# Early periods written out per engine, two small moves at the end of even periods, and small loads issued by ScalarE

## The chip, the cores and the metric

The kernel runs on one core of a Trainium2 chip. The metric is the device time of one launch in microseconds (us). Engines are named as in the profile: PE is TensorE, ACT ScalarE, DVE VectorE, POOL GpSimd; SP only issues DMAs.

## What is computed

One decoder block over 16 sequences of 128 tokens with 128 features, in float32:

```
x = LN(x + mixer(x))        # projection to 3x128, causal convolution of 3 taps on each channel,
                            # k*v, causal convolution of 4 taps, q*(..), projection to 128
x = LN(x + xattn(x, ctx))   # self attention (16 heads of 64), LN, cross attention to ctx, LN,
                            # feed forward 128-512-128 with GELU, LN
x = LN(x + ffn(x))          # 16 experts for tokens 0 to 15, one shared network for the rest
```

Both attentions mask keys by one padding mask.

## The kernel before, in words

All work sits in two blocks of hand-written instruction lists, one list per engine; engines meet only through semaphores, and an engine runs its list strictly in order. `mixer_and_attentions` (L263) holds the mixer and both attentions, `feed_forward` (L1057) the rest. A matmul that must be exact runs as three (`mm_split`, L71) over a high and a low part, so each operand is first split: ACT writes the high part, DVE the low part by a subtraction.

The first block is a loop over **periods** `p`, the same loop in all four engines, from `FIRST = -9` to 32. Period p works on attention item p (self attention of sequence p, and from 16 on cross attention of sequence p-16): values `v_half(p)`, four `unit`s (two head pairs of queries or keys each, for two sequences at once, needed by items two periods ahead), `transposes(p-1)` of the probabilities, `out_proj(p-2)`, `scores(p+1)`, `p_v(p-1)`. ACT does `exps`, `q_out`, `v_out`, `ot_out`; DVE `maxima` (with the mask), `reciprocals`, `k_out`, `pt_out`, `residual`, `xT_low`; POOL `normalise`, `affine` and the powers that make inverse deviations.

The mixer works on pairs m = 0 to 7 of sequences and is spread over the same periods, by leads that `pair_of(p, lead)` (L341) turns into a pair:

```
PROJECT, CONVOLVE, OUTPUT, TRANSPOSE = 8, 6, 5, 4
```

So pair m is projected at p = 2m-8 and 2m-7 (`projection`, 9 matmuls for each of 3 parts, evicted by `projected` into `C`), convolved at p = 2m-6 (POOL `keys_values` the period before, DVE `inner_convolution` L841, POOL `gate` L996), sent through the output matmul at 2m-5 (`mixer_output`, DVE `mixer_residual` and `mixer_statistics`, POOL `mixer_deviation`, DVE `mixer_shift`), and normalised and transposed at 2m-4 (ACT `mixer_normal` L655, PE `x1_transposes` L543, ACT `x1_high`, DVE `x1_low` L883). `x1T` is what the units read. Pair 0 reaches its transposes at p = -4; the units begin at p = -2 and `scores(0)` (L455) stands at the end of p = -1. The weights of self attention are split at p = -5, -4 and -3, and the mask is cast on DVE at p = -2 (L928).

In an even period with a pair to convolve (p = 0, 2, 4, 6, 8 of the periods from 0 on) `inner_convolution` stands on DVE right after `normalise(p-3)` and ahead of the reciprocals and copies of the period, and `gate` on POOL ahead of the four `normalise(p, g)`. `mixer_residuals` (L1018) stands at the end of an odd period's list on POOL.

All loads but the mask's are issued by SP, in the order of L370 to L396.

## Time and profile before

| | |
|---|---|
| median of 3 runs | 538.31 us (537.59 to 538.4) |
| the profiled execution's own time | 538.34 us |
| its span, first to last instruction | 536.6 us |
| mean granted PE clock | 0.951 |
| scores(0) starts | 49.27 us |
| first exponential on ACT | 51.67 us |

The profiled execution lies 0.03 us from the median, and 1.74 us of its time are outside the span. Times of rows count from the span's start. "[0.43 <-DVE at_k L758]" behind a row is the time for which the engine was idle before it, and what ended that.

### The profile page before, as it was taken

The numbers are of one execution on the slowest core, as the hardware profiler recorded it, in microseconds if no ns is written. First come the engines' busy times: TensorE is split into PE (matmuls) and PEld (weight loads), VectorE is DVE, ScalarE is ACT, GpSimd is POOL, SyncE is SP. The second block draws the span as 40 slices with busy tenths as digits, with TensorE's granted clock in tenths as the row PEclk, the third lists the DMA queues.
The fourth block names the chain that finished last, engine by engine and source line by source line (L and its number), as shares of the span: only waits on it lengthen the run. The fifth ranks groups of instructions, "written<-read, shape, count | busy, mean of one in ns | idle before, by whom it ended". The sixth has DMA issues, their size and how long they took to land. (4 is left out here: it accounts for less than half of the span.)

```text
span 536.6 us, 14182 instructions
## 1 busy us (share of the span) xinstructions
PE 482.3 (90%) x4662; PEld 445.1 (83%) x4662; DVE 396.1 (74%) x1882; ACT 368.5 (69%) x1394; POOL 262.3 (49%) x349
## 2 busy tenths in 40 slices
PE   3569799999998989999999999999999998989482
PEld 2558689989897989999999999999999977879372
DVE  3555678787879888887778778877777776277864
ACT  3343877868787776888878767888877675634634
POOL 0342554564748465545544445455544455243561
PEclk9878999999999999999999999999999999997665
DMA  7840000000000000400000000000000000040003
GB/s 202 257 163 2 0 2 2 2 2 2 2 2 2 1 2 1 116 3 2 2 1 2 2 3 2 2 1 3 1 2 2 2 2 1 1 161 2 2 19 79
DMA packets 15865, 14.25 MB, mean 27 GB/s; under 512 B 2865, under 2 KB 13489, under 8 KB 15665
## 3 DMA queue, kind: packets, MB, share of 16 engines
q1 hardware_dynamic: 15648, 13.08, 8.0%
q8 instruction: 38, 0.62, 0.5%
q10 hardware_dynamic: 144, 0.26, 0.2%
q14 instruction: 35, 0.28, 0.2%
HBM read 12.16 MB, written 1.18 MB: 25 GB/s over the span
## 5 line engine op out<-in xcount | busy, mean ns | idle before, releaser
L594 ACT ACTIVATE P<-P,at_negmax 128x128 f32<-128x128 f32 x512 | 198.9, 396 | 81.2 <-DVE at_negmax L740 81.2
L955 POOL TENSOR_TENSOR P<-P,at_inv 128x512 f32<-128x512 f32 x128 | 136.5, 1077 | 122.6 <-DVE at_inv L750 122.5
L740 DVE CUSTOM_DVE_ANT_0 P<-late_bank,maskb 128x128 f32<-128x128 f32 x512 | 111.3, 287 | 0.1
L766 DVE COPY at_PT<-late_bank 128x512 f32<-128x512 f32 x128 | 87.2, 686 | 31.0 <-PE late_bank L451 30.8
L594 ACT ACTIVATION_READ_ACCUMULATOR P<-P,at_negmax 128x1 f32 x512 | 99.9, 195 | 0.0
L451 PE MATMUL late_bank<-ident,P 128*128 128x128 f32 x512 | 76.6, 273 | 4.7 <-DVE at_negmax L740 2.3
L451 PEld LDWEIGHTS late_bank<-ident,P 128*128 128x128 f32 x512 | 59.7, 140 | 11.6 <-issue 7.3
L468 PE MATMUL late_bank<-at_k,at_q 64*128 64x128 f32 x1024 | 65.8, 278 | 0.4 <-DVE at_k L758 0.4
L468 PEld LDWEIGHTS late_bank<-at_k,at_q 64*128 64x128 f32 x1024 | 59.7, 188 | 4.4 <-issue 0.7
L483 PE MATMUL late_bank<-at_PT,V 128*64 128x128 f32 x1024 | 63.0, 276 | 0.0
L483 PEld LDWEIGHTS late_bank<-at_PT,V 128*64 128x64 f32 x1024 | 55.2, 137 | 3.9
L758 DVE COPY at_k<-late_bank 128x512 f32<-128x512 f32 x64 | 44.2, 690 | 16.3 <-PE late_bank L75 15.2
L740 DVE DVE_READ_ACCUMULATOR2_ANT at_negmax<- 128x1 f32 x512 | 42.8, 84 | 0.0
L973 POOL TENSOR_TENSOR at_N<-at_N,row_ln_g 128x128 f32<-128x128 f32 x32 | 15.3, 478 | 54.9 <-DVE at_N L791 54.9
L604 ACT ACTIVATE at_q<-late_bank 128x512 f32<-128x512 f32 x64 | 37.6, 588 | 1.5 <-PE late_bank L75 1.5
L613 ACT ACTIVATE V<-late_bank 128x512 f32<-128x512 f32 x64 | 37.5, 586 | 0.0
L499 PE MATMUL late_bank<-wo_sa,at_OT 128*128 128x128 f32 x256 | 31.6, 276 | 3.6 <-DVE x1T_lo L887 3.6
L621 ACT ACTIVATE at_OT<-late_bank 128x512 f32<-128x512 f32 x64 | 34.1, 586 | 0.0
L499 PEld LDWEIGHTS late_bank<-wo_sa,at_OT 128*128 128x128 f32 x256 | 29.8, 192 | 4.6 <-issue 4.6
L525 PE MATMUL late_bank<-xT_hi,w_hi 128*128 128x256 f32 x72 | 24.6, 341 | 9.9 <-DVE xT_lo L811 8.4
L1384 POOL TENSOR_TENSOR ffrstd<-ffmv,half_neg 128x4 f32<-128x4 f32 x16 | 16.2, 1016 | 30.9 <-DVE ffmv L1277 30.9
L499 PE MATMUL late_bank<-wo_ca,at_OT 128*128 128x128 f32 x256 | 31.2, 275 | 0.0
(182 smaller groups left out, 1113.9 us busy)
## 6 DMA issues: line engine op xcount, KB each, us to landing
ctxT_raw<-in_ctxT SPq DMA_DIRECT2D x1, 1024.0 KB, 8.7
out<-xres SPq DMA_DIRECT2D x4, 224.0 KB, 2.5
x<-in_xT SPq DMA_DIRECT2D x1, 768.0 KB, 7.3
xres<-in_x SPq DMA_DIRECT2D x1, 768.0 KB, 12.2
tap_rows<-in_short_wT SPq DMA_DIRECT2D x3, 192.0 KB, 5.1
sa_wq_raw<-in_sa_wq SPq DMA_DIRECT2D x1, 512.0 KB, 4.9
sa_wk_raw<-in_sa_wk SPq DMA_DIRECT2D x1, 512.0 KB, 5.8
sa_wv_raw<-in_sa_wv SPq DMA_DIRECT2D x1, 512.0 KB, 8.1
```

Source lines behind the costliest of these rows:

```text
L451: last = nc.tensor.transpose(banks[T_BANK[g % 2]][:, h * 128:(h + 1) * 128], P[:, n % 2, HQ * g + h, :], k.ident[:])
L468: last = nc.tensor.matmul(score_bank(h), q[rows, t % 2, h // 2, pair], kk[rows, t % 2, h // 2, pair], start=True, stop=True)
L483: last = nc.tensor.matmul(banks[O_BANK[h // 8]][part:part + 64, h // 2 % 4 * 128:(h // 2 % 4 + 1) * 128], V[:, n % 2, h * DH:(h + 1) * DH] ...
L499: last = nc.tensor.matmul(banks[W_BANK][:, 0:128], OT[:, n % 2, c, :], out_w[att(n)][:, c, :], start=(c == 0), stop=(c == H // 2 - 1))
L594: last = nc.scalar.activation(P[:, n % 2, h, :], P[:, n % 2, h, :], ACT.Exp, scale=-1.0, bias=negmax[:, n % 2, h:h + 1], accum_out=total[: ...
L604: nc.scalar.activation(q[:, t % 2, u:u + 2, :], banks[UNIT_BANK[0]][:].rearrange("p (h l) -> p h l", h=2), ACT.Copy, scale=NEG_SCALE).then ...
L613: nc.scalar.activation(V[:, n % 2, half * 512:(half + 1) * 512], banks[V_BANK][:], ACT.Copy).then_inc(v_ok, 1)
L621: nc.scalar.activation(OT[:, n % 2, 4 * o:4 * o + 4, :], banks[O_BANK[o]][:].rearrange("p (c l) -> p c l", c=4), ACT.Copy).then_inc(ot_ok, 1)
L740: last = nc.vector.tensor_tensor_reduce(P[:, n % 2, h, :], score_bank(h), k.maskb[:, cols(n)], scale=1.0, scalar=3.0e38, op0=ALU.add, op1= ...
L758: nc.vector.tensor_copy(kk[:, t % 2, u - 1:u + 1, :], banks[UNIT_BANK[1]][:].rearrange("p (h l) -> p h l", h=2)).then_inc(k_ok, 1)
L766: nc.vector.tensor_copy(PT[:, HQ * g:HQ * g + HQ, :], banks[T_BANK[g % 2]][:].rearrange("p (h l) -> p h l", h=HQ)).then_inc(pt_ok, 1)
L955: nc.gpsimd.tensor_tensor(tile, tile, inv[:, n % 2, HQ * g:HQ * g + HQ].unsqueeze(2).to_broadcast([128, HQ, 128]), ALU.mult).then_inc(norm ...
```

## The change

- The periods -9 to -1 are no longer a loop: each engine has a list written out. PE runs the projections of pairs 0, 1 and 2 before any unit, all eight units of sequence pair 0 and `scores(0)` next, and the projection of pair 3 with the output of pair 2 behind `scores(0)`. The loop starts at p = 0.
- Seven small loads (taps, biases, `b_out`, `w_out`) are issued by ACT instead of SP; on SP the weights of the queries and keys move ahead of the token loads.
- From p = 0 on, DVE's `inner_convolution` stands behind `x1_low`, and POOL's `gate` behind `inverse_deviation`; POOL's `mixer_residuals` moves from the end of an odd period's list to its start.
- The mask is cast right after the first biases. `x1_transposes` waits for `x1_low` of the pair before it as well.

```
...
         ITEMS = 2 * NSEQ
-        FIRST, FIRST_UNITS = -9, -2
+        FIRST_UNITS = -2
...
-            sp.dma_start(taps[:], io["short_w"].rearrange("(c p) j -> p c j", p=128)).then_inc(ld_small, 16)
-            sp.dma_start(short_b[:], io["short_bT"]).then_inc(ld_small, 16)
-            sp.dma_start(b_in[:], io["b_inT"]).then_inc(ld_small, 16)
-            sp.dma_start(inner[:], io["inner_w"]).then_inc(ld_small, 16)
-            sp.dma_start(inner_b[:], io["inner_b"].rearrange("(p o) -> p o", o=1)).then_inc(ld_small, 16)
             sp.dma_start(xT_raw[:, seqs(1), :], io["xT"][:, seqs(1), :]).then_inc(ld_x[1], 16)
-            row_broadcast(nc, sp, b_out[:], io["b_out"]).then_inc(ld_tok, 16)
-            sp.dma_start(w_out[:], io["W_out"]).then_inc(ld_tok, 16)
+            for n in SA[:2]:
+                sp.dma_start(k.raw[n][:], io[n]).then_inc(ld_w[n], 16)
             tokens = io["x"].rearrange("b p d -> p b d")
             sp.dma_start(k.xres[:, 0:GRP], tokens[:, 0:GRP]).then_inc(ld_xres[0], 16)
-            for n in SA[:2]:
-                sp.dma_start(k.raw[n][:], io[n]).then_inc(ld_w[n], 16)
             sp.dma_start(xT_raw[:, GRP:, :], io["xT"][:, GRP:, :]).then_inc(ld_x[2], 16)
             sp.dma_start(k.raw[SA[2]][:], io[SA[2]]).then_inc(ld_w[SA[2]], 16)
             for n, tile in k.rows.items():
...
                 if m is None:
                     return
                 pe.wait_ge(n1_ok, m + 1)
+                wait(pe, x1lo, m)
                 wait(pe, xT_lo, p - 3)
                 wait(pe, r_ok, p - 2)
                 for b in range(PAIR):
...
 
             pe.wait_ge(ident_ok, 1)
             pe.wait_ge(pads_ok, 2)
-            for p in range(FIRST, ITEMS + 1):
+            for m in (0, 1):
+                for c in range(3):
+                    projection(-1, m, c)
+            mixer_output(-1, 0)
+            for c in range(3):
+                projection(-1, 2, c)
+            x1_transposes(-1, 0)
+            unit(-2, 0)
+            unit(-2, 1)
+            mixer_output(-1, 1)
+            unit(-2, 2)
+            unit(-2, 3)
+            x1_transposes(-1, 1)
+            for j in range(4):
+                unit(-1, j)
+            scores(0)
+            projection(-1, 3, 0)
+            projection(-1, 3, 1)
+            mixer_output(-1, 2)
+            projection(-1, 3, 2)
+
+            for p in range(ITEMS + 1):
                 x_transpose(p - 4)
                 v_half(p, 0)
                 unit(p, 0)
...
             zero = k.zeros[:].rearrange("p (a b c) -> p a b c", a=2, b=PAIR)
...
+            nc.scalar.dma_start(taps[:], io["short_w"].rearrange("(c p) j -> p c j", p=128)).then_inc(ld_small, 16)
+            nc.scalar.dma_start(short_b[:], io["short_bT"]).then_inc(ld_small, 16)
+            nc.scalar.dma_start(b_in[:], io["b_inT"]).then_inc(ld_small, 16)
+            nc.scalar.dma_start(inner[:], io["inner_w"]).then_inc(ld_small, 16)
+            nc.scalar.dma_start(inner_b[:], io["inner_b"].rearrange("(p o) -> p o", o=1)).then_inc(ld_small, 16)
+            row_broadcast(nc, act, b_out[:], io["b_out"]).then_inc(ld_tok, 16)
+            nc.scalar.dma_start(w_out[:], io["W_out"]).then_inc(ld_tok, 16)
             for c in range(3):
                 act.wait_ge(w3_ok, c + 1)
                 part = np.s_[:, :, c * D:(c + 1) * D]
...
                 if c == 0:
                     x_high(0)
             x_high(1)
-
-            for p in range(FIRST, ITEMS + 1):
+            for c in range(3):
+                projected(0, c)
+            x_high(2)
+            weight_high(SA[0])
+            for c in range(3):
+                projected(1, c)
+            weight_high(SA[1])
+            projected(2, 0)
+            projected(2, 1)
+            mixer_normal(0)
+            projected(2, 2)
+            x1_high(0)
+            q_out(-2, 0)
+            weight_high(SA[2])
+            mixer_normal(1)
+            q_out(-2, 2)
+            x1_high(1)
+            q_out(-1, 0)
+            x_high(3)
+            q_out(-1, 2)
+            for c in range(3):
+                projected(3, c)
+            x_high(4)
+
+            for p in range(ITEMS + 1):
                 exps(p, 0)
                 exps(p, 1)
                 xT_high(p - 4)
...
                 projected(pair_of(p, PROJECT), 1)
                 projected(pair_of(p, PROJECT - 1), 2)
                 exps(p, 3)
-                if p % 2 and p >= -5:
+                if p % 2:
                     x_high((p + PROJECT + 1) // 2)
-                if p in (-5, -4, -3):
-                    weight_high(SA[p + 5])
-                elif p in (1, 3, 5):
+                if p in (1, 3, 5):
                     weight_high(CA[p // 2])
                 elif p in (7, 9):
                     context_high((p - 7) // 2)
...
             first_weights()
             x_low(1)
             first_biases()
-            for p in range(FIRST, ITEMS + 1):
+            vec.wait_ge(ld_mask, 16)
+            nc.vector.tensor_scalar(k.maskb[:], k.mask_raw[:], MASKED, None, ALU.mult).then_inc(mask_ok, 1)
+            inner_convolution(0)
+            x_low(2)
+            weight_low(SA[0])
+            mixer_residual(0)
+            mixer_statistics(0)
+            weight_low(SA[1])
+            mixer_shift(0)
+            inner_convolution(1)
+            x1_low(0)
+            k_out(-2, 1)
+            mixer_residual(1)
+            mixer_statistics(1)
+            mixer_shift(1)
+            k_out(-2, 3)
+            weight_low(SA[2])
+            x1_low(1)
+            k_out(-1, 1)
+            inner_convolution(2)
+            x_low(3)
+            k_out(-1, 3)
+            maxima(0, 0)
+            maxima(0, 1)
+            mixer_residual(2)
+            mixer_statistics(2)
+            mixer_shift(2)
+            x_low(4)
+
+            for p in range(ITEMS + 1):
                 maxima(p, 2)
                 maxima(p, 3)
                 normalise(p - 3)
-                inner_convolution(pair_of(p, CONVOLVE))
                 reciprocals(p, 0)
                 reciprocals(p, 1)
                 xT_low(p - 4)
...
                 k_out(p, 3)
                 pt_out(p - 1, 3)
                 x1_low(pair_of(p, TRANSPOSE))
+                inner_convolution(pair_of(p, CONVOLVE))
                 mixer_residual(pair_of(p, OUTPUT))
                 mixer_statistics(pair_of(p, OUTPUT))
                 reciprocals(p, 2)
-                if p % 2 and p >= -5:
+                if p % 2:
                     x_low((p + PROJECT + 1) // 2)
-                if p in (-5, -4, -3):
-                    weight_low(SA[p + 5])
-                elif p == -2:
-                    vec.wait_ge(ld_mask, 16)
-                    nc.vector.tensor_scalar(k.maskb[:], k.mask_raw[:], MASKED, None, ALU.mult).then_inc(mask_ok, 1)
-                elif p in (2, 4, 6):
+                if p in (2, 4, 6):
                     weight_low(CA[p // 2 - 1])
                 elif p in (8, 10):
                     context_low((p - 8) // 2)
...
             nc.gpsimd.memset(k.half_neg[:], -0.5).then_inc(consts_ok, 1)
             pool.wait_ge(consts_ok, 2)
             pool.wait_ge(edge_ok, 2)
-            for p in range(FIRST, ITEMS + 1):
+            keys_values(0)
+            output_bias(0)
+            gate(0)
+            keys_values(1)
+            output_bias(1)
+            mixer_deviation(0)
+            gate(1)
+            keys_values(2)
+            mixer_residuals(0)
+            mixer_deviation(1)
+            output_bias(2)
+            gate(2)
+            mixer_residuals(1)
+            mixer_deviation(2)
+            keys_values(3)
+            output_bias(3)
+
+            for p in range(ITEMS + 1):
+                mixer_residuals(pair_of(p, TRANSPOSE - 1))
                 affine(p - 3)
                 next_residual(p - 3)
-                gate(pair_of(p, CONVOLVE))
                 for g in range(QUARTERS):
                     normalise(p, g)
                 mixer_deviation(pair_of(p, OUTPUT))
                 inverse_deviation(p - 2)
+                gate(pair_of(p, CONVOLVE))
                 keys_values(pair_of(p, PROJECT - 1))
                 output_bias(pair_of(p, PROJECT - 1))
-                mixer_residuals(pair_of(p, TRANSPOSE - 1))
 
             affine(ITEMS - 2)
             next_residual(ITEMS - 2)
```

The order that results on PE, behind the output matmul of pair 0 (`w_out,yT`) and around the transposes of pair 0 (`ident,N`). Before:

```order
L527 MATMUL late_bank<-xT_hi,w_lo 128x256
L539 MATMUL late_bank<-w_out,yT 128x128 x2
L550 MATMUL late_bank<-ident,N 128x128 x2
L525 MATMUL late_bank<-xT_hi,w_hi 128x256
L526 MATMUL late_bank<-xT_lo,w_hi 128x256
```

The change:

```order
L519 MATMUL late_bank<-xT_lo,w_hi 128x256
L520 MATMUL late_bank<-xT_hi,w_lo 128x256
L544 MATMUL late_bank<-ident,N 128x128 x2
L73 MATMUL late_bank<-x1T_hi,sa_wq_hi 128x256
L74 MATMUL late_bank<-x1T_lo,sa_wq_hi 128x256
L75 MATMUL late_bank<-x1T_hi,sa_wq_lo 128x256
```

Before, the projection of pair 2 (`xT`, `w`) follows the transposes of pair 0; now it has run by then, and the first unit (`x1T`, `sa_wq`) follows them.

On ACT, from the evictions of pair 0's projection to the first copies of queries. Before:

```order
L652 ACTIVATE C<-late_bank,conv_bias 128x256 x6
L643 ACTIVATE xT_hi<-x 128x2x128
L674 ACTIVATE sa_wq_hi<-sa_wq_raw 128x1024
L662 ACTIVATE N<-R,shift,rstd 128x128 x2
L670 ACTIVATE x1T_hi<-late_bank 128x256
L652 ACTIVATE C<-late_bank,conv_bias 128x256 x2
L674 ACTIVATE sa_wk_hi<-sa_wk_raw 128x1024
L652 ACTIVATE C<-late_bank,conv_bias 128x256
L643 ACTIVATE xT_hi<-x 128x2x128
L674 ACTIVATE sa_wv_hi<-sa_wv_raw 128x1024
L604 ACTIVATE at_q<-late_bank 128x512
```

The change:

```order
L667 ACTIVATE C<-late_bank,conv_bias 128x256 x3
L658 ACTIVATE xT_hi<-x 128x2x128
L689 ACTIVATE sa_wq_hi<-sa_wq_raw 128x1024
L667 ACTIVATE C<-late_bank,conv_bias 128x256 x3
L689 ACTIVATE sa_wk_hi<-sa_wk_raw 128x1024
L667 ACTIVATE C<-late_bank,conv_bias 128x256 x2
L677 ACTIVATE N<-R,shift,rstd 128x128 x2
L667 ACTIVATE C<-late_bank,conv_bias 128x256
L685 ACTIVATE x1T_hi<-late_bank 128x256
L619 ACTIVATE at_q<-late_bank 128x512
L689 ACTIVATE sa_wv_hi<-sa_wv_raw 128x1024
L677 ACTIVATE N<-R,shift,rstd 128x128 x2
```

The high parts of the weights stand further ahead between evictions (`C`), and all evictions of pair 2 stand ahead of the first copy of queries (`at_q`) with only the normalisation `N` between them.

On DVE in period 4, from the end of `maxima(4, 3)` to the reciprocals. Before:

```order
L791 TENSOR_SCALAR at_N<-at_R,at_mv,at_rstd 128x128
L847 TENSOR_SCALAR G<-KV,inner,inner_b 128x256
L851 SCALAR_TENSOR_TENSOR G<-KV,inner,G 128x256 x3
L750 RECIPROCAL at_inv<-at_total 128x4 x2
L798 TENSOR_TENSOR x1T_lo<-late_bank,x1T_hi 128x128
L766 COPY at_PT<-late_bank 128x512
L758 COPY at_k<-late_bank 128x512
```

Further on in the same period, with the change:

```order
L801 COPY at_k<-late_bank 128x512
L809 COPY at_PT<-late_bank 128x512
L930 TENSOR_TENSOR x1T_lo<-late_bank,x1T_hi 128x256
L890 TENSOR_SCALAR G<-KV,inner,inner_b 128x256
L894 SCALAR_TENSOR_TENSOR G<-KV,inner,G 128x256 x3
L793 RECIPROCAL at_inv<-at_total 128x4
L935 TENSOR_TENSOR ca_wk_lo<-ca_wk_raw,ca_wk_hi 128x1024
L821 TENSOR_TENSOR at_R<-late_bank,xres 128x128
```

The four instructions of the convolution (`G<-KV`) stood ahead of the copies of probabilities and keys (`at_PT`, `at_k`); now they stand behind these and behind `x1_low` (`x1T_lo`, 256 wide), and ahead of the third reciprocal, the weight's low part and the residual `at_R`.

## Rows read from the trace of the kernel before

**Rows 1.** Busy time and granted clock by stretch: stretch, then engines, PEclk, DMA

```profile
0.00:49.27 49.27, 29.14 (x172) 27.43 (x173) 23.44 (x52) 17.79 (x36) 12.18 (x25) 0.86 0.53 170
...
80.00:440.00 360.00, 354.15 (x3707) 330.09 (x3708) 288.39 (x1413) 279.39 (x1141) 192.96 (x256) 1.00 0.03 6
```

**Rows 2.** Timeline of PE, 24 to 50 us: start us, us, what [idle before <-releaser]

```profile
24.40 0.69 PE L550 MATMUL late_bank<-ident,N 128*128 128x128 f32 x2 [3.98 <-ACT N L662]
...
30.82 0.37 PE L73 MATMUL late_bank<-x1T_hi,sa_wq_hi 128*128 128x256 f32 x1
...
31.79 0.36 PE L73 MATMUL late_bank<-x1T_hi,sa_wk_hi 128*128 128x256 f32 x1
...
38.64 0.69 PE L550 MATMUL late_bank<-ident,N 128*128 128x128 f32 x2 [4.73 <-ACT N L662]
...
49.27 2.06 PE L468 MATMUL late_bank<-at_k,at_q 64*128 64x128 f32 x32 [0.43 <-DVE at_k L758]
```

**Rows 3.** Timeline of DVE, 11 to 39 us

```profile
11.78 0.16 DVE L830 TENSOR_TENSOR tap_b<-taps,b_in 128x9 f32<-128x9 f32 x1
...
20.46 0.42 DVE L860 TENSOR_TENSOR R<-late_bank,xres 128x256 f32<-128x256 f32 x1 [1.63 <-PE late_bank L539]
...
22.13 1.22 DVE L892 TENSOR_TENSOR sa_wq_lo<-sa_wq_raw,sa_wq_hi 128x1024 fp32r<-128x1024 f32 x1
23.27 0.17 DVE L880 SCALAR_TENSOR_TENSOR shift<-mv,rstd 128x2 f32<-128x2 f32 x1
24.25 0.80 DVE L847 TENSOR_SCALAR G<-KV,inner,inner_b 128x256 f32<-128x256 f32 x1 [0.82 <-POOL KV L994]
25.08 1.53 DVE L851 SCALAR_TENSOR_TENSOR G<-KV,inner,G 128x256 f32<-128x256 f32 x3
...
38.31 0.68 DVE L758 COPY at_k<-late_bank 128x512 f32<-128x512 f32 x1
```

**Rows 4.** Timeline of ACT, 6 to 52 us

```profile
6.85 0.52 ACT L689 ACTIVATE w_hi<-w_raw 128x384 fp32r<-128x384 f32 x1 [4.07 <-DVE w_raw L820]
...
23.47 0.88 ACT L662 ACTIVATE N<-R,shift,rstd 128x128 f32<-128x128 f32 x2 [2.88 <-DVE shift L880]
...
47.73 0.47 ACT L652 ACTIVATE C<-late_bank,conv_bias 128x256 f32<-128x256 f32 x1 [0.48 <-PE late_bank L527]
...
51.67 0.40 ACT L594 ACTIVATE P<-P,at_negmax 128x128 f32<-128x128 f32 x1 [3.16 <-DVE at_negmax L740]
```

**Rows 5.** Timeline of POOL, 18 to 23 us

```profile
18.91 0.73 POOL L1001 TENSOR_TENSOR yT<-C,G 128x256 f32<-128x256 f32 x1 [1.79 <-DVE G L851]
21.97 0.82 POOL L1016 TENSOR_TENSOR rstd<-mv,half_neg 128x2 f32<-128x2 f32 x1 [2.33 <-DVE mv L874]
```

**Rows 6.** Busy time and granted clock in one early microsecond

```profile
23.00:24.00 1.00, 0.00 (x0) 0.00 (x0) 0.43 (x2) 0.53 (x2) 0.92 (x2) 0.69 0.91 270
```

**Rows 7.** One small load's issue, and loads with their us to landing

```profile
5.74 0.43 SPq L380 DMA_DIRECT2D inner_b<-in_inner_b  x1
...
row_ln_b<-in_ln_b SPq DMA_DIRECT2D x2, 64.0 KB, 9.1
...
inner_b<-in_inner_b SPq DMA_DIRECT2D x1, 0.5 KB, 3.1
```

**Rows 8.** Timeline of PE in periods 4 and 5

```profile
110.70 0.41 PE L550 MATMUL late_bank<-ident,N 128*128 128x128 f32 x2 [0.22 <-issue]
...
115.53 2.02 PE L499 MATMUL late_bank<-wo_sa,at_OT 128*128 128x128 f32 x16 [0.28 <-DVE x1T_lo L887]
...
124.08 0.39 PE L73 MATMUL late_bank<-sa_wv_hi,x1T_hi 128*128 128x512 f32 x1
```

**Rows 9.** Timeline of DVE in period 4

```profile
108.22 2.05 DVE L851 SCALAR_TENSOR_TENSOR G<-KV,inner,G 128x256 f32<-128x256 f32 x3
...
117.59 0.29 DVE L778 TENSOR_TENSOR at_R<-late_bank,xres 128x128 f32<-128x128 f32 x1 [1.01 <-PE late_bank L499]
```

**Rows 10.** Timeline of ACT in period 5

```profile
122.91 0.58 ACT L613 ACTIVATE V<-late_bank 128x512 f32<-128x512 f32 x1
```

## The prediction

> **What bounds the kernel now.** Time can come only from stretches in which PE, the busiest engine, idles or runs at its low clock, so the windows are read first. From 80 to 440 us PE is busy 354.15 of 360 us at clock 1.00: nothing but 5.85 us is left there. Up to 49.27 us, the start of the first scores, it is busy 29.14 us at a mean clock of 0.86: 20.1 us idle, and some of the busy time at half speed [rows 1]. This is the stage that the change rewrites.
>
> What is late there is read from PE's own timeline. The transposes of pair 0 start at 24.40 after 3.98 us idle, the first unit only at 30.82, the transposes of pair 1 at 38.64 after 4.73 us idle, the first scores at 49.27 [rows 2]. The idle times wait for the chain gate, output matmul, residual, statistics, power on POOL, shift, `N` on ACT [rows 3 to 5]; and while it waits, PE has projections in its list that stand behind the transposes and so cannot fill the gap. The clock falls with it: it is granted 1.00 up to about 23.7 us, after three idle us, and 0.69 on average in the next microsecond [rows 6], so the projection of pair 2 then runs at the lower of the two levels.
>
> **Startup, step by step.** I follow the new lists from POOL's gate of pair 0, which ends at 18.91 + 0.73 = 19.64 [rows 5]. Ahead of it the lists hold the same work in the same order; the mask's cast falls into DVE's wait for the first `KV`, the split of the query weights behind the first convolution ends before the residual is ready, and the high parts of weights fit between evictions. I cost these at nothing.
>
> 1. Output of pair 0, residual at 20.46, power at 21.97 to 22.79 as before. DVE splits a weight in this wait (1.22 us at 22.13), as it did before, and makes the shift at 23.27 [rows 3, 5]. `N` takes 0.88 us on ACT [rows 4], so the transposes are at 24.4, no gain. But PE now projects pair 2 (27 matmuls) between 20.2 and 23.7, where it sat idle.
> 2. On DVE the convolution of pair 1 follows the shift: 0.80 + 1.53 = 2.3 us [rows 3], then `x1_low` (0.42, as the residual, which has its shape), done at 26.1. The first unit starts then, not at 30.82: 4.7 us earlier.
> 3. Two units of 0.97 us (30.82 to 31.79 [rows 2]) and the output of pair 1 end at 28.4. Copy of keys 0.68, from the residual to the power's start 1.5 and the power 0.8 [rows 3, 5], shift 0.17, `N` 0.88, with 0.05 to 0.1 at each hand-over: the transposes of pair 1 at 32.5, against 38.64.
> 4. The copy of queries behind `N` (0.6, as the copy of `V` [rows 10]), two more units, the copy of keys (0.68), then on DVE the convolution of pair 2 (2.3), `xT` low (0.42), the last copy of keys (0.68): 39.4. The scores start 9.9 us earlier.
> 5. What was ahead of the scores is now behind them: scores 2.0, two parts of the projection of pair 3 at 1.1 (9 matmuls each where a unit has 6), an eviction (0.47 [rows 4]) that the output of pair 2 waits for, that output 0.4, the third part 1.1, its eviction 0.47, `xT` high 0.4, and hand-overs of 0.5: the first exponential runs at 46.9 instead of 51.67 [rows 4]. So only 4.8 of the 9.9 us are left. With fewer hand-over costs (steps 3 and 4 have 12 at 0.1 or less) it is 5.6. I take **5.1 us**.
>
> From the first exponential on, period 0 is held by ACT (exponentials, then the copy of `V` for which PE waits), in the old list and in the new one; the 5.1 us pass on unchanged. The convolution of period 0 now lies in DVE's wait for ACT's last exponentials.
>
> **The loads.** One issue takes 0.43 us [rows 7]; seven of them plus one slow one end near 6.4 us on ACT, which waits until 6.85 for DVE anyhow [rows 4]. SP's 3 us less of issuing serve loads that nobody waits for. I put zero, and up to 2.7 us for a late bias (a rival below).
>
> **Even periods (2, 4, 6, 8).** Removed: PE's waits of 0.22 for the transposes of a pair (ACT had waited for `mixer_residuals`, which now run half a period earlier, in POOL's idle time) and of 0.28 at `out_proj` for `x1_low` [rows 8]. In periods 4 and 6 both, in 2 one: 1.3 us.
> Added: DVE now does the convolution where it has only 1.01 us to spare, its wait before the residual `at_R` at 117.59 [rows 9]. 2.3 - 1.0 = 1.3 us late are the residual and, queued behind it, `maxima(p+1)`, the exponentials that wait for them, and the copy of `V` behind these on ACT. That copy ended at 122.91 + 0.58 = 123.49 and PE reads its bank's successor at 124.08: 0.6 us of slack [rows 8, 10]. PE loses 0.7 in each of four periods: 2.8 us. Bounds: 0 if DVE's wait grows because `x1_low` comes early, and 4 x 1.3 = 5.2 if nothing absorbs it. The gate behind `inverse_deviation` is read a period later and costs nothing. Net of the even periods: **+1.5 us**.
>
> The convolution's own length is unsure: its last three instructions took 1.53 us in the startup and 2.05 in period 4, where POOL worked on other tiles beside it [rows 3, 9]. The Trainium skill (SBUF — State Buffer, Who interferes with whom) says that a VectorE instruction with two SBUF inputs and a GpSimd one that reads SBUF keep each other out for a whole instruction. By that rule, with which the trace's 2.05 agrees, one meeting with POOL's normalisation of about 1 us in the new place would make it 3.3 us, the loss per period 1.7 and the sum 538.7, which is the direction of the rival on DVE below.
>
> **Sum.** 538.34 - 5.1 + 1.5 = 534.7 us for an execution like the profiled one, which stands at the median (538.31).
>
> **Rivals.**
> - *The moves in the loop cost nothing.* DVE's spare time takes the convolution whole, and startup hands on 5.6: 538.3 - 5.6 - 1.3 = 531.4. For: DVE is busy 288 of 360 us in the loop [rows 1]. Against: the 1.01 us of [rows 9] is all that stands right there. 0.13.
> - *PE's clock falls once more in the startup.* There still are waits of about 2 us, before step 3's transposes and before the scores; the trace shows the fall only after three [rows 6]. A spell at the low level from 26 us on costs up to 0.6 us in each of the four units on the chain (0.97 us [rows 2], most of it matmuls that take twice as long): 2.4, so 537.1. 0.10.
> - *The small loads land late.* The row loads took 9.1 us when the queue was full, against 3.1 for `inner_b` [rows 7]. Issued at 5.4 and taking 9.1, they would be there at 14.5, 2.7 us after DVE reads them now (11.78 [rows 3]): 537.4. The Trainium skill (DMA: Bandwidth & Descriptors, Queues, rings and completion order) says that each DMA engine goes round between the queues that have work; by that a small load on ACT's queue does not wait for SP's megabyte, and the sum stays 534.7. No run here shows it yet. 0.08.
> - *DVE becomes the bound in even periods*, the case on the other side. The convolution takes 2.9 us beside POOL, `maxima(p+1, 1)` and `(p+1, 3)` come late for the unit and the transposes of the next period too, and PE waits for 2.3 us or more in each of four periods: 538.3 - 5.1 + 9.2 = 542.4. It decides from 1.3 us lost per period, where 5.1 is used up. Against it: 0.6 us of slack are measured [rows 8, 10], and DVE idles later in each odd period. 0.07.
> - *The startup gives nothing in the end*: every gain up to the scores is taken back in periods 0 and 1, whose lists hold more of ACT's work at once. 538.3. Against: the first exponential is what ACT starts from. 0.07.
>
> **The numbers.** The forecast has 0.55, with 533 to 536 as its own range. About 0.2% (1.1 us) is what a measurement of this kernel can tell from no change, so faster means below 537.2. To it go the forecast, the first rival, and parts of the second and third (0.06 and 0.04): 0.78. Within 0.2%: the rest of these two and the last rival, 0.15. Slower: 0.07. For 8 in 10 the range reaches from the first rival, 531.2, to the third, 537.6.
>
> **What would show it.** Right: scores at 39 to 40 us, the first exponential at 46 to 47.5, granted clock 1.00 from 13 us on; in even periods no wait before `x1_transposes`, a wait of PE of 0.5 to 1 us before the second `V` half of the odd period, DVE's 1.01 us before `at_R` gone. Wrong: a first exponential later than 49; a clock of 0.5 between 24 and 44 us; a conv_bias later than 12.7; PE waits over 1.3 us in odd periods, which would make the kernel slower; or none at all there, which would make it nearly 3 us faster than I say.

## The result, and the profile after

The changed kernel takes 531.87 us (median of 15 runs, 530.23 to 535.25) against 538.24 us (15 runs) of the kernel before beside it. The ratio of the means is 0.9901 with a 95% interval of 0.9882 to 0.9920, that is 5.3 us less (4.3 to 6.4); by the medians it is 6.4. It is faster by well over 0.2%, and the median lies in the range, 0.7 us from its lower end; the forecast of 534.7 was 2.8 us too high.

The profiled execution took 530.23 us, the fastest of the 15, with a span of 528.4 and a mean granted clock of 0.968. Busy time by stretch, of the kernel after (columns as in [rows 1]: the length, the busy us of PE, of its weight loads, of DVE, ACT and POOL with the number of instructions, then the granted clock, the share of the DMA engines and GB/s):

```profile
0.00:40.73 40.73, 23.23 (x142) 21.52 (x142) 23.34 (x51) 16.08 (x32) 12.24 (x26) 0.92 0.63 205
40.73:56.66 15.93, 12.96 (x114) 12.05 (x114) 7.27 (x46) 9.67 (x36) 5.69 (x8) 1.00 0.01 2
80.00:440.00 360.00, 354.54 (x3731) 330.45 (x3730) 289.21 (x1445) 279.02 (x1147) 192.76 (x257) 1.00 0.02 6
433.74:528.40 94.66, 70.25 (x554) 61.81 (x553) 62.56 (x290) 47.10 (x119) 41.05 (x50) 0.85 0.13 38
```

and of the kernel before, two stretches, from scores(0) to scores(1) and from scores(31) to the end:

```profile
49.27:60.10 10.83, 9.30 (x83) 8.25 (x83) 8.86 (x50) 8.05 (x32) 6.55 (x9) 1.00 0.01 2
...
438.69:536.60 97.91, 74.36 (x554) 65.66 (x553) 62.31 (x290) 47.09 (x119) 40.96 (x50) 0.80 0.12 36
```

The start of scores(n) on PE is the ruler of what follows, since everything in the loop passes through it:

| start of | before | after | difference |
|---|---|---|---|
| scores(0) | 49.27 | 40.73 | -8.54 |
| scores(1) | 60.10 | 56.66 | -3.44 |
| scores(3) | 88.49 | 85.03 | -3.46 |
| scores(4), (5) | 101.87, 117.48 | 98.54, 113.35 | -3.33, -4.13 |
| scores(6), (7) | 130.92, 146.52 | 127.03, 141.84 | -3.89, -4.68 |
| scores(8), (9) | 159.96, 174.45 | 155.51, 169.24 | -4.45, -5.21 |
| scores(11) to (31) | 200.54 to 438.69 | 195.58 to 433.74 | -4.96, -4.95 |
| end of the span | 536.6 | 528.4 | -8.2 |

Three parts are to be read off: 3.4 us from the startup, which is what is left of 8.5 after 5.1 are lost again between scores(0) and scores(1); 1.5 us from periods 3 to 9, where the even ones gain 0.80, 0.79 and 0.76 and the odd ones give back 0.13 to 0.24; and 3.2 us behind scores(31), where the change has touched nothing.

The startup on PE after the change, answering to [rows 2]:

```profile
20.83 0.61 PE L532 MATMUL late_bank<-w_out,yT 128*128 128x128 f32 x4
...
26.20 0.44 PE L544 MATMUL late_bank<-ident,N 128*128 128x128 f32 x2 [1.08 <-ACT N L677]
27.57 0.39 PE L73 MATMUL late_bank<-x1T_hi,sa_wq_hi 128*128 128x256 f32 x1 [0.93 <-DVE x1T_lo L930]
...
33.79 0.69 PE L544 MATMUL late_bank<-ident,N 128*128 128x128 f32 x2 [2.66 <-ACT N L677]
...
40.73 2.06 PE L461 MATMUL late_bank<-at_k,at_q 64*128 64x128 f32 x32 [1.93 <-DVE at_k L801]
...
51.97 0.50 PE L73 MATMUL late_bank<-sa_wv_hi,x1T_hi 128*128 128x512 f32 x1 [2.31 <-ACT V L628]
```

The first row is the output product of pair 0, which PE began at 19.74 before. For the next four I had forecast 24.4, 26.1, 32.5 and 39.4. They are 1.8, 1.5, 1.3 and 1.3 us late: the error is made before the transposes at 26.20 and then only carried. DVE and POOL there (answering to [rows 3, 5]), first DVE, then POOL:

```profile
6.73 0.56 DVE L863 TENSOR_TENSOR w_raw<-w_in,tap_rows 128x384 f32<-128x384 f32 x1 [6.73 <-DMA tap_rows<-in_short_wT]
...
19.74 1.76 DVE L935 TENSOR_TENSOR sa_wq_lo<-sa_wq_raw,sa_wq_hi 128x1024 fp32r<-128x1024 f32 x1
21.48 0.42 DVE L903 TENSOR_TENSOR R<-late_bank,xres 128x256 f32<-128x256 f32 x1
...
22.74 0.60 DVE L917 TENSOR_SCALAR mv<-mv 128x2 f32<-128x2 f32 x1
23.25 1.21 DVE L935 TENSOR_TENSOR sa_wk_lo<-sa_wk_raw,sa_wk_hi 128x1024 fp32r<-128x1024 f32 x1
...
25.07 0.16 DVE L923 SCALAR_TENSOR_TENSOR shift<-mv,rstd 128x2 f32<-128x2 f32 x1 [0.61 <-POOL rstd L1083]
```

```profile
23.42 1.62 POOL L1083 TENSOR_TENSOR rstd<-mv,half_neg 128x2 f32<-128x2 f32 x1
```

DVE's first step waits for the tap rows until 6.73 instead of 6.25. The residual of pair 0 (`R`) starts at 21.48 instead of 20.46, right behind the split of `sa_wq`, which takes 1.76 us instead of 1.22 with POOL's gate beside it, and the power starts at 23.42 instead of 21.97. It then takes 1.62 us instead of 0.82, with the split of `sa_wk` beside it. On ACT, answering to [rows 4]:

```profile
44.10 0.47 ACT L667 ACTIVATE C<-late_bank,conv_bias 128x256 f32<-128x256 f32 x1 [5.71 <-PE late_bank L520]
...
48.26 0.39 ACT L609 ACTIVATE P<-P,at_negmax 128x128 f32<-128x128 f32 x1
```

The first exponential comes at 48.26, 3.4 us earlier than before; I had said 46.9. Of the clock, the two low stretches of the startup after the change, which cost 1.7 us of full speed each (length times one minus the clock):

```profile
16.00:20.00 4.00, 3.97 (x21) 4.00 (x22) 2.77 (x6) 1.78 (x4) 2.06 (x4) 0.57 0.57 133
33.00:37.00 4.00, 3.21 (x16) 3.02 (x17) 1.98 (x3) 2.51 (x6) 0.00 (x0) 0.57 0.00 0
```

Period 4 after the change, DVE and then PE, answering to [rows 8, 9]:

```profile
111.17 0.40 DVE L890 TENSOR_SCALAR G<-KV,inner,inner_b 128x256 f32<-128x256 f32 x1
111.61 1.52 DVE L894 SCALAR_TENSOR_TENSOR G<-KV,inner,G 128x256 f32<-128x256 f32 x3
...
114.25 0.28 DVE L821 TENSOR_TENSOR at_R<-late_bank,xres 128x128 f32<-128x128 f32 x1
```

```profile
111.40 0.80 PE L492 MATMUL late_bank<-wo_sa,at_OT 128*128 128x128 f32 x5 [0.28 <-DVE x1T_lo L930]
```

It is PE's only wait in the period. The one before the transposes of x1 is gone, and so is one of 0.19 us before the third `transposes` of P that I had not priced. Counted from scores(4), the first start 0.38 us earlier than before (8.45 us behind it instead of 8.83) and the second 0.76 (8.67 instead of 9.43): that is the whole gain of the period, more than the idle times in the rows say. The 0.28 at `out_proj`, which I had taken off, is still there.

### The profile page after: what moved, and what is told of

Same layout as the page of the kernel before. It is cut to its first block and busy times, and to the rows that moved or that the text cites. A ratio compares the mean times of both kernels' runs of the same rounds, so it can differ in the third digit from the quotient of the medians.

```text
span 528.4 us, 14189 instructions
## 1 busy us (share of the span) xinstructions
PE 475.4 (90%) x4662; PEld 439.3 (83%) x4662; DVE 394.4 (75%) x1882; ACT 368.0 (70%) x1394; POOL 261.4 (49%) x349
## 5 line engine op out<-in xcount | busy, mean ns | idle before, releaser
L518 PE MATMUL late_bank<-xT_hi,w_hi 128*128 128x256 f32 x72 | 23.3, 323 | 10.8 <-DVE xT_lo L854 8.9
L492 PEld LDWEIGHTS late_bank<-wo_ca,at_OT 128*128 128x128 f32 x256 | 29.9, 192 | 0.1
```

The costliest lines, as they stand in the source:

```text
L492: last = nc.tensor.matmul(banks[W_BANK][:, 0:128], OT[:, n % 2, c, :], out_w[att(n)][:, c, :], start=(c == 0), stop=(c == H // 2 - 1))
```

## The experiments

Twelve kernels ran. The theory after the result was: the startup is worth 3.4 us because of ACT's order and PE's clock, the loop 1.5 because of a collision, and the end is the clock's. Each kernel was timed beside the kernel before on the same chip. The first four shared their runs of before (median 538.5).

### The moves in the loop alone

The kernel before, with the four moved calls of the loop written as in the changed kernel, for p >= 0 only.

```
                 x1_low(pair_of(p, TRANSPOSE))
+                if p >= 0:
+                    inner_convolution(pair_of(p, CONVOLVE))
...
                 inverse_deviation(p - 2)
+                if p >= 0:
+                    gate(pair_of(p, CONVOLVE))
```

and so for `mixer_residuals`, at the head of the period.

> The startup and loads of the kernel before; only the moves in the loop from period 0 on (convolution and gate to the end of even periods' lists, mixer_residuals to the start of odd ones). Theory A, read from the two traces: no shift against before up to scores(3), then 0.6 us gained by each of periods 4, 6 and 8, about 1.5 us in all by scores(12); a run near 536.7 us. Theory B, my forecast's term: each even period costs PE 0.7 us, so scores(12) come 1.5 us late and the run is near 539.7 us. If the last 90 us of the program are shorter than before here too or not, as the clock falls, that is chance and no effect of the moves.

534.88 us median of 10 runs, ratio 0.9949 (0.9923 to 0.9974), 2.7 us less (1.4 to 4.1). In its trace scores(1) starts 0.69 us earlier than in the kernel before, though all ahead of it is unchanged, and scores(12) 2.17: the moves give 1.5 us, as in the full change and as theory A had it. The rest of the 2.7 us is not theirs by this trace.

### The startup lists and loads alone

The changed kernel with convolution, gate and residuals back at their old places.

```
                 normalise(p - 3)
+                inner_convolution(pair_of(p, CONVOLVE))
...
                 x1_low(pair_of(p, TRANSPOSE))
-                inner_convolution(pair_of(p, CONVOLVE))
```

> The written-out early lists and the loads issued by ScalarE, with the loop as before from period 0 on. Theory A: the first scores near 41 us and the first exponential near 48.3 us, 3.4 us early, and the same 3.4 us at scores(12): a run near 534.8 us. Theory B (the early lists change what periods 4 to 8 wait for, too): a shift of 4.9 us at scores(12) and a run near 533.3 us, and then the moves in the loop would be worth nothing.

536.5 us median of 12 runs (533.3 to 539.52), ratio 0.9974 (0.9951 to 0.9997), 1.4 us less (0.2 to 2.6). The trace says why it is so little: scores(0) starts at 40.47, a little earlier than in the full change, and scores(1) at 59.58 instead of 56.66, from the same lists. Ahead of scores(0), at it and ahead of scores(1) lie low stretches, where the profiled execution of the full change had its own at 16 and 33 us; windows of this kernel:

```profile
26.00:31.00 5.00, 4.07 (x23) 3.86 (x22) 1.95 (x5) 2.00 (x4) 3.00 (x5) 0.66 1.04 415
40.00:44.00 4.00, 3.54 (x32) 3.52 (x32) 1.52 (x10) 0.00 (x0) 1.67 (x3) 0.57 0.00 0
54.00:58.00 4.00, 4.00 (x22) 3.95 (x21) 0.94 (x4) 3.56 (x14) 2.73 (x3) 0.57 0.00 0
```

So with the same startup lists the clock falls at other places in another execution. From scores(3) to scores(12) nothing is gained here (-0.49 us at both): all of the loop's 1.5 us is from the moves.

### Small loads back on SP

```
-            nc.scalar.dma_start(taps[:], ...)
+            sp.dma_start(taps[:], ...)
```

and so for all seven, in SP's old order, so that the weights of queries and keys are issued late again too.

> The changed kernel with the seven small loads issued by SP again, in the old order of loads. Theory A: sharing the DMA engines with the taps' row loads is what made the first one land at 6.7 instead of 6.25 us; on SP it is 6.25 again, and the load of the later x, issued 1.5 us later, may make ACT wait longer than the 1.03 us it waits now: the first exponential between 0.5 us earlier and 0.7 us later, the whole within 0.7 us of the changed kernel. Theory B (the issue on ScalarE is what feeds the startup): bias or x come late and the first exponential is over 1.5 us later than 48.3.

532.96 us median of 6 runs, ratio 0.9898 (0.9863 to 0.9933): no difference that can be told from the full change. The first `w_raw` starts at 6.36 instead of 6.73 and the first eviction at 12.90 instead of 13.44, so the new loads do delay the head by about half a microsecond (the first `w_raw` starts at 6.24 to 6.36 us in the four traces with the old loads, at 6.52 to 7.24 in the ten with the new). Whether by ScalarE's queue or by the weights issued 4 us earlier on SP, no run separates. Scores(0) comes at 40.11 instead of 40.73. The gain is gone by scores(1) (57.57), with a low stretch at 53 to 56 us ahead of it.

### The split of the second weight moved away from POOL's power

```
-            weight_low(SA[1])
             mixer_shift(0)
             inner_convolution(1)
             x1_low(0)
+            weight_low(SA[1])
```

> The changed kernel with DVE's low part of the key weights (1.2 us) moved from ahead of the first mixer_shift to behind the first x1_low. Theory A: beside it POOL's power took 1.62 us where it takes 0.71 alone, and the last statistics instruction 0.60 instead of 0.17; moved, the power takes 0.7 to 0.8, the shift of pair 0 is at 24.0 instead of 25.07, the first unit starts 1.0 us earlier and the first exponential 0.8 us earlier. Theory B (the power's length has nothing to do with DVE): the power stays at 1.6, the shift moves by less than 0.3 and the split delays the first key unit.

533.79 us median of 6 runs, ratio 0.9904 (0.9878 to 0.9930). The power is short again, in this kernel's timeline of POOL and PE:

```profile
23.54 0.71 POOL L1083 TENSOR_TENSOR rstd<-mv,half_neg 128x2 f32<-128x2 f32 x1
```

```profile
25.41 0.44 PE L544 MATMUL late_bank<-ident,N 128*128 128x128 f32 x2 [0.64 <-ACT N L677]
```

The transposes start 0.8 us earlier although PE's first matmul came 0.5 us later in this execution (9.43 against 8.92). So the split beside it made the power 0.9 us longer, and this is about half of my 1.8 us. The power takes 1.61 or 1.62 us in all eight traces with the split there and 0.71 in the three without. Scores(0) comes no earlier (40.96): a 0.63 us wait for the split now stands before the second unit, and the clock was low from 33 to 40 us.

### Convolution, gate and residuals back, one at a time

Three kernels, one run each: the changed kernel with one of the three calls at its old place.

> The changed kernel with the inner convolution alone back at the place it had (after the normalisation, ahead of the first reciprocals of a period); gate and residuals stay moved. Read by the start of scores(n) on TensorE, period by period, where the changed kernel's even periods are 0.80 us shorter than those of the kernel before and its odd periods 0.13 to 0.24 us longer. Theory A (the 2 us of convolution ahead of the copies of the transposed probabilities made these copies late, and with them TensorE's wait before the third quarter's transposes): the even periods get back 0.4 us, about half of the 0.80, and the waits of 0.19 us before the transposes of P are there again; the wait before the transposes of x1 stays away. Theory B (the convolution ran in VectorE's idle time in either place, and the gain is the residuals' alone): no even period changes by over 0.1 us. Theory C (all three moves only work together): all of the 0.80 us comes back.

> The changed kernel with GpSimd's gate alone back behind the next residual, where it now waits for a convolution that VectorE does only late in the period. Theory A (GpSimd's list stands still at the gate until VectorE has done the convolution, and norm, bias and keys behind it are late): the even periods become at least 1 us longer than in the changed kernel, since the inverse deviation and the affine of the next items stand behind it. Theory B (GpSimd has idle time enough in even periods, some 5 us of it before the norm): no period changes by over 0.1 us. Both read by the start of scores(n) on TensorE.

> The changed kernel with the mixer residuals alone back at the end of odd periods. Theory A (the residuals read N and held up ScalarE's next normalisation, and with it TensorE's transposes of x1): TensorE's wait of 0.22 us before these transposes is back and the even periods get back 0.4 us, the other half of the 0.80. Theory B (the wait of 0.22 us belonged to the convolution too): no change over 0.1 us per pair of periods. It may also gain: the residuals now delay GpSimd's affine at the head of even periods by 1.4 us, and if the odd periods' 0.13 to 0.24 us are from that, they go away.

The single times were 534.47, 531.71 and 535.05 us. By the ruler, from scores(3) to scores(12), against the kernel before:

| kernel | conv. moved | residuals moved | gate moved | even periods 4, 6, 8 | sum to scores(12) |
|---|---|---|---|---|---|
| startup alone | no | no | no | 0.0 | 0.0 |
| convolution back | no | yes | yes | -0.72, -0.72, -0.73 | -2.17 |
| residuals back | yes | no | yes | -0.80, -0.79, -0.76 | -1.52 |
| gate back | yes | yes | no | -0.80, -0.79, -0.75 | -1.48 |
| full change | yes | yes | yes | -0.80, -0.79, -0.76 | -1.50 |

Neither half of the 0.80 belongs to one move, as my expectations had it: with the gate moved, the residuals' move alone brings 0.72 and the convolution's alone all of it, and taking the gate back changes nothing. No kernel moved the gate alone or left it behind with only one of the others. What the two moves have in common is that they part the convolution on DVE from the residuals on POOL. With neither moved (the startup's lists alone), DVE and then POOL in period 4:

```profile
106.85 0.83 DVE L890 TENSOR_SCALAR G<-KV,inner,inner_b 128x256 f32<-128x256 f32 x1
107.71 2.06 DVE L894 SCALAR_TENSOR_TENSOR G<-KV,inner,G 128x256 f32<-128x256 f32 x3
```

```profile
106.81 0.72 POOL L1093 TENSOR_TENSOR xres<-N,row_sa_bo 128x256 f32<-128x256 f32 x1
107.49 0.78 POOL L1093 TENSOR_TENSOR x<-N,row_ln_b 128x256 f32<-128x256 f32 x1
```

and with the convolution back but the residuals gone from there, DVE:

```profile
105.55 0.40 DVE L890 TENSOR_SCALAR G<-KV,inner,inner_b 128x256 f32<-128x256 f32 x1
105.99 1.77 DVE L894 SCALAR_TENSOR_TENSOR G<-KV,inner,G 128x256 f32<-128x256 f32 x3
```

Beside the residuals the convolution takes 2.9 us from its start to its end, without them 2.2 and in the new place 2.0. The 0.7 us push back what DVE does behind it, the low part of x and then the copies of P. PE waits for the first with the transposes of x1 (0.53 us later, counted from scores(4)) and for the second with the third transposes of P (0.20 more), and that is the 0.72. ACT's wait for the residuals ahead of `N` is not the cause: it is 0.38 us with neither moved and still 0.32 with the residuals back, where the period gains its full 0.80. The Trainium skill's rule (SBUF — State Buffer, Who interferes with whom) that a VectorE instruction with two SBUF inputs and a GpSimd one that reads SBUF keep each other out agrees with these rows; I had used it against the new place, where POOL idles, and not for the old one.

What moving the convolution adds is a loss in odd periods (0.13 to 0.24 us; none with it back), while DVE works off the convolution and a weight's split ahead of the next item's residual. In the change's trace that residual starts 0.90 us behind scores(5) instead of 0.11, the next exponentials on ACT 0.68 later (2.86 instead of 2.18), the copy of V behind them too, and PE's second half of V comes out 0.25 late. This is the path that I had forecast, at 0.7 us. So the old place, without the residuals beside it, is the better one by 0.67 us between scores(3) and scores(12).

The gate shows how much room POOL has: back at its old place it stands still for 7.5 us, and nothing is late.

```profile
114.60 1.71 POOL L1068 TENSOR_TENSOR yT<-C,G 128x256 f32<-128x256 f32 x1 [7.50 <-DVE G L894]
```

### The first exponentials ahead of projection 3's evictions

```
+            exps(0, 0)
             projected(3, 0)
             projected(3, 1)
+            exps(0, 1)
             projected(3, 2)
```

> The changed kernel with ScalarE's first two groups of exponentials moved ahead in its startup list: exps(0,0) before projected(3,0), exps(0,1) before projected(3,2), nothing else changed. In the changed kernel's trace the first group's maxima are ready at 43.1 us, and ScalarE starts the exponentials at 48.3, behind three bias steps of projection 3 that wait for TensorE. Theory A (this order holds the first exponential, and is why scores(0) came 8.5 us earlier and scores(1) only 3.4): first exponential at about 43.2 us, the copy of V's first half at 48.2 instead of 51.3, TensorE's wait of 2.3 us before V's second half gone, scores(1) at 53.5 to 55 instead of 56.7, median 529 to 530.5. Theory B (the exponentials are bound by VectorE's maxima 2 and 3 and by GpSimd's norm anyway): first exponential early, scores(1) within 0.5 us of 56.7, median 531 to 532.5. Theory C (projection 3's late bias steps hold up TensorE and with it everything): scores(1) later than 57.

532.5 us median of 6 runs (529.18 to 532.88), ratio 0.9904 (0.9877 to 0.9930). The first exponential came at 45.71, 3.45 us behind scores(0), not 7.5:

```profile
45.71 0.40 ACT L609 ACTIVATE P<-P,at_negmax 128x128 f32<-128x128 f32 x1 [5.55 <-DVE at_negmax L787]
```

Scores(0) itself was late (42.26) and slow (3.67 us instead of 2.06) in a low stretch from 42 to 45 us, so this trace alone doesn't settle it. Two kernels below have a clock of 1.00 from scores(0) to scores(1): 15.94 us between them in the order of the change (with idle work), 14.90 with the exponentials ahead (all together). The exponentials come 2.5 us behind scores(0) there (42.55), not 7.5, and these 5.0 us bring 1.0. But that kernel also does the convolution of period 0 at its old place, and PE waits 1.25 us for a copy of keys that stands behind it. Here, without that, it is 14.98 us from scores(0) to scores(1) though scores(0) ran 1.61 us slow; at full clock it might be 13.4 (an estimate, 14.98 - 1.61, if all of that passes on). So the exponentials' place is worth 1.0 to 2.6 us, and how much of the 2 to 3 that I expected is there stays open.

### Idle work in the startup's waits, after and before

Transposes of the identity that nobody reads, so that TensorE doesn't stand still; in both kernels.

```
+            warm(14)
             x1_transposes(-1, 1)
```

> The changed kernel with idle work for TensorE in its startup waits: 5, 3, 6, 5, 14, 10, 3 and 12 transposes of the identity into columns nobody reads, ahead of projections (1,0) and (1,1), the transposes of x1 of pair 0, unit 0, the transposes of pair 1, scores(0), the output product of pair 2 and V's second half of item 0. Nothing else is changed and nothing is waited for more. Theory A (the startup's gain of 3.4 us at scores(1), and the spread between profiles of the same startup, 0.5 to 3.4 us, come from the granted clock falling after TensorE's waits): the granted clock stays at 1.00 from 12 to 60 us, scores(1) at 56.0 to 56.7 us, median of the runs under that of the changed kernel by 0.5 to 1.5 us: 530.5 to 531.4. Theory B (the clock's falls have nothing to do with the waits): it falls all the same, scores(1) anywhere from 56.7 to 59.6. Theory C (the added transposes delay the real work): clock 1.00, and scores(0) later than 41.5 us.

> The kernel before with the same idle work in its own startup waits: 4, 3, 5, 22, 26 and 6 transposes of the identity, ahead of projections (1,0) and (1,1), the output product of pair 0, the transposes of x1 of pairs 0 and 1, and V's second half of item 0. With it and the run of the changed kernel with idle work the startup's two orders stand against each other at the same clock. Theory A (the new order is worth about 4 us at the same clock and the low clock took some of it): the granted clock stays at 1.00, the low stretches of 23.7 to 30.1 and 37.5 to 43.6 us are gone, scores(1) moves from 60.1 to 57 to 58.5, and the new order's lead over it with idle work on both is 1 to 2 us. Theory B (the order alone makes the lead, the clock takes alike from both): scores(1) at 59.5 to 60 here, lead 3.4 us with idle work too. Median 535.5 to 537 by A, 538 by B.

With the change: 532.55 us median of 5 runs, ratio 0.9904 (0.9883 to 0.9925). Without it: 535.24 us median of 10 runs, ratio 0.9950 (0.9926 to 0.9974), 2.7 us less than the kernel before. So the change gains nothing from the idle work. Windows of the first, then of the second:

```profile
12.00:60.00 48.00, 41.33 (x335) 37.95 (x334) 30.42 (x107) 24.48 (x71) 18.84 (x26) 1.00 0.35 122
```

```profile
12.00:38.00 26.00, 20.84 (x154) 19.75 (x153) 15.35 (x37) 10.09 (x20) 10.48 (x16) 1.00 0.66 233
38.00:42.00 4.00, 3.91 (x20) 3.91 (x21) 0.65 (x2) 1.39 (x4) 0.66 (x1) 0.57 0.00 0
42.00:60.00 18.00, 16.70 (x155) 15.29 (x155) 12.48 (x55) 11.64 (x42) 7.57 (x10) 1.00 0.01 3
```

The old startup gains from the idle work: scores(1) at 58.77 instead of 60.10, with one of its two low stretches gone; the other, after a wait of 2.28 us that the idle work left over, costs 1.7 us of full speed still. The new one stays at 56.63, where its profiled execution was. This does not say that its two low stretches cost nothing, for the start was worse here: the view shows 1.00 where the trace has no record yet, and by the matmuls of 128x256, which start 0.21 us apart up to 17.7 us and 0.12 after it, PE was at its low level till then, against 12.8 us in the change's own trace, and the residual of pair 0 came at 22.68 instead of 21.48. The kernel before with idle work leaves the low level at 17.9 us, so these two compare. With idle work in both the lead of the new lists is 2.1 us instead of 3.4, and if the stretch of 38 to 42 us were gone as well perhaps under 1 (58.77 - 1.7 = 57.1 against 56.63, an estimate). So a part of what the new startup gains is that PE stands still less and drops its clock less; by the estimate it is most, which no run shows. The median that I expected of the first, 530.5 to 531.4, was missed by over 1 us; its scores(1) and scores(31) (433.75) stand where they stood, and what differs from the change's profiled execution is the end (next part).

### All together, and the end

The convolution back, the exponentials ahead, the split moved, idle work in the startup; then the same with idle work in the waits of `feed_forward` too.

```
             def shared_w1(g):
+                idle_work((10, 22, 14, 0)[g])
                 pe.wait_ge(z_lo, g + 1)
```

> The changed kernel with four edits together: the inner convolution back at its old place in the loop; ScalarE's first two groups of exponentials ahead of projection 3's bias steps; the split of the second weight behind x1's low part of pair 0, away from GpSimd's power; idle transposes in TensorE's startup waits (8, 3, 5, 7, 20, 14 and 4, none ahead of V's second half, which no longer waits). By the theory each part adds its own gain, worked out from the traces: loop between scores(3) and scores(12) 0.67 us shorter than in the changed kernel (as with the convolution back alone); exponentials about 2 us (scores(1) at 54 to 55 instead of 56.7, with the clock at 1.00); the split up to 0.8 us more. scores(12) at 204.0 to 205.5 instead of 207.5, median 529.5 to 530.5. Rival: the early gain meets another bound by scores(1) (GpSimd's norm, VectorE's maxima), scores(12) at 206.5 to 207 and the median 531 to 532.5.

> The kernel of the run before it, with idle transposes in the waits of the feed-forward end as well: 10, 22 and 14 ahead of the first product of groups 0 to 2, 15 and 9 ahead of the second product of groups 0 and 1, into a bank that is free by then. Theory A (the stretch behind scores(31), 94.7 us in the profiled run of the changed kernel and 97.9 in that of the kernel before, differs by the granted clock, which falls to 0.50 behind TensorE's waits there): the clock stays at 1.00 behind 494 us, the stretch takes 90 to 92.5 us, and the median is 3 us or more under that of the run before it. Theory B (the end is bound by VectorE, ScalarE and GpSimd, whatever the clock): the stretch stays at 94 to 96.5 us. Theory C (the clock falls although TensorE is kept busy, as at 482 us, where it was): the stretch stays at 94 to 96.5 us with the clock at 0.50 in it.

530.25 us median of 5 runs, ratio 0.9844 (0.9819 to 0.9870), and 529.51 us median of 4 runs, ratio 0.9834 (0.9814 to 0.9855). Both beat the changed kernel (0.9901). The parts added up as far as scores(12): 205.13 instead of 207.50 in the change, of which 0.6 by the convolution, 1.0 by the exponentials and 0.7 by the rest ahead of scores(0). Behind the exponentials PE now waits for DVE, which does the maxima up to 50.2 us and then the convolution, back at its old place, up to 52.1 (timeline of PE, without idle work in the end):

```profile
52.91 0.39 PE L73 MATMUL late_bank<-x1T_hi,sa_wk_hi 128*128 128x256 f32 x1 [1.25 <-DVE at_k L816]
```

The end, of the first and then of the second:

```profile
488.00:513.00 25.00, 15.71 (x73) 12.92 (x73) 20.73 (x88) 12.23 (x28) 16.50 (x16) 0.65 0.05 10
431.38:528.00 96.62, 73.05 (x554) 64.29 (x553) 62.62 (x290) 47.14 (x119) 40.99 (x50) 0.81 0.13 37
```

```profile
488.00:513.00 25.00, 19.22 (x146) 16.58 (x144) 20.66 (x89) 12.53 (x28) 17.03 (x16) 1.00 0.04 8
432.13:527.10 94.97, 75.29 (x624) 66.92 (x623) 62.40 (x290) 47.07 (x119) 40.99 (x50) 0.93 0.13 38
```

The idle work keeps the clock at 1.00 from 488 to 513 us, and its end is 1.65 us shorter than that of the kernel beside it, not the 3 and more of theory A. Nor is it shorter than the 94.7 us that the change had without idle work, so with one trace of each the 1.65 may be the draw as well, and by the medians, 0.7 us apart with ratios whose intervals overlap, no gain of the idle work in the end is shown. That the chain over DVE, POOL and ACT is what bounds the end now is my reading and was not tried. Its four runs lie closer together, 528.97 to 529.66 against 528.26 to 530.65 in five. (Its scores(31) came 0.75 us later, after a low stretch at 60 us.)

Over all profiles the stretch behind scores(31), the same instructions in all but the last, has three lengths: 94.7 us (the change, the loop alone, gate back; clock 0.85 to 0.86), 96.5 to 96.6 (seven kernels; 0.81 to 0.82) and 97.8 to 97.9 (the kernel before, the startup alone, convolution back; 0.80 to 0.82). Kernels with and without the moves in the loop are in the middle group and in the last, so the change doesn't set the length. What goes with it is where the clock's first fall behind scores(31) lands: 48.9 to 49.4 us behind it in the three longest, where the low stretch also lasts twice as long, 50.0 to 50.3 in the three shortest, 50.4 to 51.6 in the seven others. The shortest came only in kernels with the moves, three of ten; whether the moment of arrival there tilts the draw stays open.

## Why the prediction was right, and where it was not

The direction was right; the steps were right in kind more than in size, and errors of both signs met in the sum. The startup gave less than forecast and the loop and the end gave more, so that the median is within 2.8 us of the forecast is partly luck.

- **Step 1, "residual at 20.46, power at 21.97 to 22.79 as before", failed.** The transposes of pair 0 came at 26.2, not 24.4. About half of it is the power. In the old list a split ran beside it too, but began 0.16 us behind it, and the power took 0.82; now the split of `sa_wk` begins first (23.25 against 23.42), and the power takes 1.62 us, where it takes 0.71 with the split moved away, as that run shows. The other half was there before the power began, at 23.42: the tap rows came 0.4 to 0.5 us late, for which the run with the loads on SP speaks (6.36 against 6.73), and the residual 1.0 (21.48). Its output product started 1.1 us late behind PE's own projections, part of which ran in the low stretch at 16 us, and the split of the query weights, which I had ending ahead of the residual, ended at 21.50. How the last half microsecond divides between these two, which end together, no run shows. I had costed the loads at nothing, and the edit at nothing that puts splits beside POOL's gate and its power.
- **Steps 2 to 4 held**: from the first transposes to scores(0) the sum said 15.0 us and the trace shows 14.5.
- **Step 5 held in the sum, not in what it assumed.** From scores(0) to the first exponential it said 7.5 us, and it was 7.53. And what it won passed on to scores(1) unchanged, 3.4 us, as forecast. But that the first exponential alone binds what follows did not hold in full: put 5.0 us earlier, it brought 1.0, at most 2.6 by the estimate above. The forecast of 5.1 us measured 3.4 in the profiled execution; over the five profiles with the new startup scores(1) lies at 58.4 on average and over the two with the old at 59.8, a lead of only 1.3, as the run of the startup alone says (1.4, 0.2 to 2.6).
- **The rival of the clock was on the right track and priced too low.** It had PE's clock fall "once more", 2.4 us, at 0.10. It falls in the startup of all ten profiled kernels without idle work, before and after, at other places each time; scores(1) ranges over 3.0 us with the same lists (56.66 to 59.65). The rise to the high level differs too: 12.8 us in the change's trace, 21.2 in that with the gate back, whose scores(0) came at 42.07. The sign "granted clock 1.00 from 13 us on" thus failed, and "a clock of 0.5 between 24 and 44 us", which was to speak against the forecast, came (33 to 37 us), as did a `conv_bias` later than 12.7 (13.34, mostly by the late tap rows and not by a late bias). And it falls after shorter waits than I had read off: 0.60 at 16 us after two waits of 1.04 and 0.66.
- **The even periods had the wrong sign**: +1.5 forecast, -1.5 measured. The convolution took 2.0 us in the new place and not 2.3. The path of the loss was right: DVE's wait before the residual is gone, the residual is 0.8 us late, and so are the exponentials and the copy of V (0.7). But of the four losses of 0.7 us on PE only 0.13 to 0.24 arrived, in odd periods, and the wait of 0.5 to 1 us that I gave as a sign did not show. The removed waits of 0.22 were there, but for another reason than the list of ACT: the convolution and the residuals stretched each other, which the 2.05 against 1.53 us of [rows 3, 9] had shown. These rows told me the cost of the collision, and I carried it to the new place in place of taking it off the old.
- **The rival "the moves in the loop cost nothing"** forecast 531.4, next to the median, and its mechanism for the loop was nearly right; but it had the startup hand on 5.6 us, which no run bears out: its number is luck.
- **The rival of the small loads** was right in kind and cost nothing by itself: `inner_b` took 8.1 us to land from ScalarE's queue, where it took 3.1 from SyncE's, with the weights issued from SyncE beside it; that a small load is free of SyncE's there, my reason against the rival, is not borne out. None was late: `b_in` was there by 7.6 us and read at 12.44.
- **Not in the sum at all**: the end, 3.2 us shorter in the profiled execution, with the clock at 0.85 instead of 0.80. Of the 5.3 us of the ratio, the averages over the profiles account for 1.3 in the startup and 1.5 in the loop; the two edits timed apart give 1.4 and 2.7, in sum 4.1 with wide intervals. How much of the remaining 1.2 or 2.5 us is the end's clock, and whether the change favours it, these runs don't settle.

## What to carry to other kernels

When a list is rewritten, price what each moved instruction stands beside on the other engines, in the place that it leaves as well as in the one it comes to: parting two operations that stretched each other was all of the loop's gain, and putting two together was about half of what the startup's first part lost. Where single profiles of one and the same list differ by 3 us, measure from mark to mark within a trace, take parts that the edit doesn't touch as the measure of chance, and hold the clock up with idle work in both kernels before crediting an order with the difference. An engine that starts earlier is worth only what the next bound leaves: scores(0) came 8.5 us earlier and scores(1) 3.4.
